# A transformer layer on eight cores: value weights loaded by halves of their columns, and the ternary scales taken at the end of two head pairs

## The chip, the cores and the metric

The kernel runs on the 8 NeuronCores of one Trainium2 chip. Every core does the whole layer for one of eight sequences, and no data passes between the cores. The metric is the device time of the slowest core in microseconds. Each core has five engines with an instruction queue of their own: PE (TensorE, matrix products), DVE (VectorE), ACT (ScalarE), POOL (GpSimd) and SP (SyncE, which only issues transfers here). The program is written engine by engine; engines wait for each other through semaphores, and nothing reorders the instructions of a queue.

## The reference

One pre-norm layer on x of 8 x 2048 x 1024: causal attention of 16 heads of 64, then a feed-forward part with quantized weights.

```python
x = x + attn(layernorm(x), W_query, W_key, W_value)      # causal softmax, 16 heads
x = x + ffn(layernorm(x), w1, conv_w, conv_b, w2)

def weight_quant(w):
    scale = 1.0 / clip(mean(abs(w)), 1e-05)
    return clip(round(w * scale), -1, 1) / scale          # ternary weights
def bit_linear(x, w):                                     # x by act_quant: 8 bits per token
    return einsum('bsd,hd->bsh', act_quant(x), weight_quant(w))
# ffn: h = bit_linear(x, w1); depthwise conv of width 3 over tokens; silu; bit_linear(h, w2)
```

## The kernel before

Tokens are worked in 16 tiles of 128 (`st` is the tile). The time falls into three stages.

**Values and first projections (0 to 104 us).** For each tile of x, DVE takes mean and variance (`moments`, L1218 to L1226), ACT forms the normalized tile `lnst` (`norm1`, L1019 to L1034, two buffers), PE turns it (`turn_ln`, L705, into `psTr`, two buffers), and DVE places it in `ln1T` (`place_ln`, L1231). PE then multiplies it by the value weights `Wvb` (`values`, L723): 8 matmuls for the left 512 columns (`nh` 0, heads 0 to 7) and 8 for the right ones. The results go round three PSUM banks `psV`; DVE copies the left half out (`place_v`, L1241), ACT the right half (`place_v`, L1049), both into `vaug`, whose columns of ones POOL writes once (L608). After every fourth tile PE projects a 512-token chunk to queries (`psQK`) and keys (`psK`) of the first head pair (`project`, L748).

The value weights are four transfers of 1 MB, each 256 rows of W_value by all 1024 columns (`load_wv`). Of each, ACT casts the first 128 rows to bf16 (L1041) and POOL the second (L597). `values` waits for all eight casts. SP issues the transfers in the order idbf, x0, wv0, wv1, x1, wv2, wv3, x2, x3, six constants, x4 to x15.

The query and key weights go another way. POOL itself issues their transfers (`load_wqk`, L502) into one staging buffer `wqkst`, casts them to bf16 (`cast_wqk`, L510 and L511), and only then issues the next one. The first issue stands in POOL's queue between its third and its fourth cast of value weights; `project` of the keys (`w` 1) waits for the second `cast_wqk`.

**Attention (104 to 468 us).** Eight head pairs (`hp` 0 to 7) of 40 slots each; slot `s` is one unit of 128 keys by up to 512 queries. In a slot PE forms scores (L806, from pair 3 on with a masking matmul L816), part of the next pair's projection (L748) and the weighted sum of an earlier unit (L834); ACT takes the exponential (L1110). Beside this DVE works through the feed-forward weights: 32 steps that sum absolute values (L1318), then 32 that make ternary weights (L1326, L1331), eight steps in a pair. The sums of each weight matrix become a scale in six small pieces: DVE `sum_columns` (L1338), PE `weight_sum` (L784), DVE `mean_weight` (L1344, L1348), PE `spread_scale_w` (L789, L791), DVE `place_scale` (L1353 to L1357). The PSUM bank `psN` that they use is shared with the norms of queries and keys, of which PE takes two sets in each pair (`norms`, L763, at slots 3 and 23, numbered `d`). So `norms(6)` and `norms(10)` wait until the scale is read out.

**Feed-forward (468 to 976 us).** 64 blocks of first products (L950), convolution on three engines, and second products (L968). The change doesn't touch this stage.

The order around the change is written out by hand in each engine's queue: the loops over `st` and over `slot` with comparisons against fixed slot numbers.

Of the kernel before, what the change touches and what calls it, by code (L numbers as in the profile page):

```python
# [16 lines left out]
S = 2048  # L17
D = 1024
# [37 lines left out]
def build_program():  # L56
# [24 lines left out]
    with es:  # L81
# [180 lines left out]

        BEFORE = {7: 0, 9: 1, 12: 2, 13: 3, 14: 4, 15: 5}
# [13 lines left out]
        def wv_quarter(n):  # L277

            return wvst[:, 2 * n * D:2 * (n + 1) * D]
# [84 lines left out]
        def _(e):  # L364
# [4 lines left out]
            def load_wv(n):  # L369
                e.dma_start(  # L370
                    out=wv_quarter(n).rearrange("p (c d) -> p c d", d=D),
                    in_=wv_h[256 * n:256 * (n + 1), :]
                    .rearrange("(c p) d -> p c d", p=128)
                ).then_inc(d_wv[n], 16)
# [122 lines left out]
        def _(e):  # L497
# [95 lines left out]
            def cast_wv(n):  # L593

                e.wait_ge(d_wv[n], 16)
                at = (2 * n + 1) * D
                e.tensor_copy(Wvb[:, at:at + D],  # L597
                              wvst[:, at:at + D]).then_inc(g_wv, 1)

            cast_wv(0)  # L600
            cast_wv(1)
# [5 lines left out]
            ap = vaug[:].rearrange("p (s h w) -> p (s h) w", h=H, w=VW)  # L607
            e.memset(ap[:, :, DH:DH + 1], 1.0).then_inc(g_vones, 1)  # L608
# [89 lines left out]
        def _(e):  # L698
# [10 lines left out]
            def values(st):  # L709
                e.wait_ge(v_lnT, st + 1)  # L710
                e.wait_ge(a_wv, 4)
                e.wait_ge(g_wv, 4)
                for nh in range(2):
                    n = 2 * st + nh
                    if n >= 3:

                        m = n - 3
                        if m % 2 == 0:
                            e.wait_ge(v_v, m // 2 + 1)
                        else:  # L720
                            e.wait_ge(a_v, m // 2 + 1)
                    for kc in range(8):
                        inst = e.matmul(  # L723
                            psV[n % 3][:],
                            ln1T[:, S * kc + 128 * st:S * kc + 128 * (st + 1)],
                            Wvb[:, D * kc + 512 * nh:D * kc + 512 * (nh + 1)],
                            start=(kc == 0), stop=(kc == 7))
                    inst.then_inc(t_v, 1)
# [25 lines left out]
            def norms(d):  # L754

                e.wait_ge(g_sq, 4 * (d + 1))
                if d >= 1:
                    e.wait_ge(a_c, d)
                if d in (6, 10):

                    e.wait_ge(v_fin, 3 if d == 6 else 6)
                for k in range(16):
                    inst = e.matmul(psN[:, k:k + 1],  # L763
                                    sqb[:, 128 * k:128 * (k + 1)],
                                    onesb[:, 0:1], start=True, stop=True,
                                    skip_group_check=True)
                inst.then_inc(t_nrm, 1)
# [13 lines left out]
            def weight_sum(f):  # L781
                e.wait_ge(v_fin, 3 * f + 1)
                e.wait_ge(a_c, 6 if f == 0 else 10)
                e.matmul(psN[0:1, 308:309], onesf[:, 0:1], smalls[:, 30:31],  # L784
                         start=True, stop=True).then_inc(t_fin, 1)
# [112 lines left out]
            for slot in range(NU + 6):  # L898
# [112 lines left out]
        def _(e):  # L1011
# [27 lines left out]
            def cast_wv(n):  # L1039
                e.wait_ge(d_wv[n], 16)  # L1040
                e.activation(out=Wvb[:, 2 * n * D:(2 * n + 1) * D],  # L1041
                             in_=wvst[:, 2 * n * D:(2 * n + 1) * D],
                             func=AF.Identity).then_inc(a_wv, 1)

            def place_v(st):
                n = 2 * st + 1
# [154 lines left out]
        def _(e):  # L1201
# [35 lines left out]
            def place_v(st):  # L1237
                n = 2 * st
# [220 lines left out]
            for slot in range(NU + 8):  # L1459
# [260 lines left out]
```

## Time and profile before

| | us |
|---|---|
| median of 3 runs | 978.73 (978.38 to 979.12) |
| the profiled execution | 977.3 |
| its span on the slowest core (core 5) | 975.7 |
| spans of all cores | 969.7 to 975.7 |
| PE / DVE / ACT / POOL busy in it | 889.0 / 711.9 / 697.3 / 620.6 |

The time of an execution is 1.6 us longer than the span of its slowest core. Share of busy time says which engine is full over the whole span (PE, 91%), not what holds it up in a given microsecond; for that the rows further down show, for single instructions, when they start, how long they take, and in square brackets how long their engine sat idle before them and what ended the wait. Unless a group says otherwise they are of core 5.

### The profile page before, as it was taken

The numbers are of one execution on the slowest core, as the hardware profiler recorded it, in microseconds if no ns is written. First come the engines' busy times: TensorE is split into PE (matmuls) and PEld (weight loads), VectorE is DVE, ScalarE is ACT, GpSimd is POOL, SyncE is SP. The second block draws the span as 40 slices with busy tenths as digits, with TensorE's granted clock in tenths as the row PEclk, the third lists the DMA queues.
The fourth block names the chain that finished last, engine by engine and source line by source line (L and its number), as shares of the span: only waits on it lengthen the run. The fifth ranks groups of instructions, "written<-read, shape, count | busy, mean of one in ns | idle before, by whom it ended". The sixth has DMA issues, their size and how long they took to land.

```text
span 975.7 us, 24133 instructions; the slowest of 8 cores (969.7 to 975.7 us)
## 1 busy us (share of the span) xinstructions
PE 889.0 (91%) x7516; PEld 538.3 (55%) x7516; DVE 711.9 (73%) x1173; ACT 697.3 (71%) x1108; POOL 620.6 (64%) x819
## 2 busy tenths in 40 slices
PE   1999899999999989998776699999999999999998
PEld 0454454555554545554654466666666666666443
DVE  2677665566666676669588988989899887877651
ACT  3554698889887888988988678678777777766300
POOL 2220648574655565545546978979799797978650
PEclk9999999999998999999989899999999999999999
DMA  8952666765876777774894323325343223332121
GB/s 262 331 169 91 233 222 214 237 215 181 255 247 218 223 243 250 231 238 191 243 313 162 108 67 118 139 92 173 109 133 128 89 94 124 108 130 88 44 87 44
DMA packets 38891, 166.93 MB, mean 171 GB/s; under 512 B 4977, under 2 KB 5106, under 8 KB 30066
## 3 DMA queue, kind: packets, MB, share of 16 engines
q1 hardware_dynamic: 34354, 148.62, 47.0%
q0 software_dynamic: 4416, 16.78, 5.1%
q8 instruction: 66, 1.08, 0.4%
q14 instruction: 55, 0.45, 0.2%
HBM read 140.22 MB, written 25.17 MB: 170 GB/s over the span
## 4 chain that ended last, share of the span: by engine, by line
PE 75%; DVE 7%; ACT 6%; issue 6%; DMA 3%; POOL 2%; SPq 0%; DVEq 0%; ACTq 0%; POOLq 0%
PE psO L968 21%; PE psM L950 19%; PE psQK L748 11%; PE psS L806 7%; PE psPV L834 6%; PE psV L723 5%; ACT PT L1110 4%; DMA wvst<-wv 2%; DMA w1b<-t1scr 2%; PE psS L816 1%; DVE psD L1543 1%; DVE hs L1524 1%; POOL hs L667 1%; PE psK L748 1%; ACT hs L1159 1%
## 5 line engine op out<-in xcount | busy, mean ns | idle before, releaser
L1110 ACT ACTIVATE PT<-psS,nbias 128x1024 bf16<-128x1024 f32 (+1 forms) x320 | 299.9, 986 | 45.2 <-PE psS L806 27.2
L950 PE MATMUL psM<-xqT,w1b 128*128 128x258 bf16 x2048 | 242.9, 277 | 20.3 <-DVE hs L1524 16.2
L667 POOL TENSOR_TENSOR hs<-hs,tb 128x256 f32<-128x256 f32 x256 | 194.6, 784 | 68.2 <-DVE hs L1524 61.8
L950 PEld LDWEIGHTS psM<-xqT,w1b 128*128 128x128 fp8e4 x2048 | 200.7, 99 | 61.4 <-issue 24.3
L1159 ACT ACTIVATE hs<-psM,convb_s,convw_s 128x256 f32<-128x256 f32 x256 | 147.5, 576 | 86.2 <-PE psM L950 61.4
L676 POOL TENSOR_TENSOR hs<-hs,srow 128x256 f32<-128x256 f32 x240 | 178.5, 777 | 15.5 <-ACT srow L1177 15.4
L1524 DVE SCALAR_TENSOR_TENSOR hs<-psM,convw_s,hs 128x256 f32<-128x256 f32 x256 | 114.8, 476 | 23.7 <-ACT tb L1163 22.6
L1543 DVE TENSOR_REDUCE psD<-hs 128x256 f32<-128x1024 f32 x56 | 109.3, 1952 | 22.0 <-ACT hs L1170 22.0
L748 PE MATMUL psQK<-ln1T,wqkb 128*128 128x512 bf16 x480 | 124.0, 382 | 1.4 <-ACT qkO L1086 0.2
L1163 ACT ACTIVATE tb<-psM,convw_s 128x256 f32<-128x256 f32 x256 | 123.6, 483 | 0.0
L834 PEld LDWEIGHTS psPV<-vaug,PT 128*128 128x128 bf16 x2176 | 92.1, 98 | 50.8 <-issue 25.5
L968 PE MATMUL psO<-w2T,hqa 128*128 128x512 fp8e4 x512 | 115.1, 379 | 0.6 <-DVE hqa L1590 0.6
L968 PE MATMUL psO<-w2T,hqb 128*128 128x512 fp8e4 x512 | 114.6, 379 | 0.0
L545 POOL TENSOR_TENSOR x<-x,ctx 128x128 f32<-128x128 f32 x128 | 82.6, 674 | 49.4 <-DVE ctx L1308 49.2
L834 PE MATMUL psPV<-vaug,PT 128*128 128x65 bf16 x2176 | 110.2, 195 | 3.1 <-DVE ctx L1308 1.3
L525 POOL TENSOR_TENSOR sqb<-qkE 128x512 bf16<-128x512 bf16 x32 | 36.8, 1150 | 74.1 <-DVE qkE L1249 51.0
L968 PEld LDWEIGHTS psO<-w2T,hqa 128*128 128x128 f16 x512 | 49.9, 98 | 56.2 <-issue 1.0
L968 PEld LDWEIGHTS psO<-w2T,hqb 128*128 128x128 f16 x512 | 50.1, 98 | 55.7
L1170 ACT ACTIVATE hs<-hs 128x1024 f32<-128x1024 f32 x64 | 68.8, 1075 | 15.6 <-POOL hs L667 15.5
L1318 DVE TENSOR_REDUCE smalls<-wbuf 128x1 f32<-128x2048 f32 x32 | 72.7, 2279 | 3.3 <-DMA wbuf<-w1q 2.1
L748 PEld LDWEIGHTS psQK<-ln1T,wqkb 128*128 128x128 bf16 x480 | 38.6, 97 | 51.3 <-issue 20.6
L806 PE MATMUL psS<-qkO 64*128 64x512 bf16 (+3 forms) x320 | 57.3, 353 | 9.7 <-ACT PT L1110 8.4
(147 smaller groups left out, 1052.8 us busy)
## 6 DMA issues: line engine op xcount, KB each, us to landing
wbuf<-w1q SPq DMA_DIRECT2D x32, 1024.0 KB, 6.3
wbuf<-w2p SPq DMA_DIRECT2D x32, 1024.0 KB, 6.7
w1b<-t1scr SPq DMA_DIRECT2D x64, 512.0 KB, 3.5
x<-x SPq DMA_DIRECT2D x16, 512.0 KB, 16.7
wqkst<-wqk POOLq DMA_DIRECT2D x16, 512.0 KB, 6.6
x1scr<-x POOLq DMA_DIRECT2D x4, 2048.0 KB, 10.0
x1g<-x1scr SPq DMA_DIRECT2D x16, 512.0 KB, 4.5
out<-x1g SPq DMA_DIRECT2D x16, 512.0 KB, 2.9
```

What stands on the lines that cost most here:

```text
L667: e.tensor_tensor(hs_quad(q)[:, part], hs_quad(q)[:, part], tb_quad(q)[:, part], ALU.add).then_inc(g_add, 1)
L676: inst = e.tensor_tensor(part, part, srow[:, at:at + GRP], ALU.mult)
L748: inst = e.matmul(bank[:], wqkb[:, at:at + 128], ln1T[:, x0:x0 + 512], start=(kc == 0), stop=(kc == 7))
L806: inst = e.matmul(bP[:, 512 * h + 128 * j:512 * (h + 1)], qk[64 * h:64 * (h + 1), k0:k0 + 128], qk[64 * h:64 * (h + 1), q0:q0 + n], start= ...
L834: inst = e.matmul(psPV[:, 512 * h + VW * m:512 * h + VW * (m + 1)], pt_unit(u)[:, p0:p0 + 128], vaug[:, v0:v0 + VW], start=(kc == 0 and m ...
L950: inst = e.matmul(psM[j][:, 0:GRP + 2], w1b[:, at:at + 128], xqT[:, x0:x0 + GRP + 2], start=(kc == 0), stop=(kc == 7))
L968: inst = e.matmul(psO[n][:], hq_of(g)[:, at:at + 128], w2T[:, D * kc + 512 * n: D * kc + 512 * (n + 1)], start=(kc == 0), stop=(kc == 31))
L1110: e.activation(out=pt_unit(u).rearrange("p (h w) -> p h w", w=512)[:, :, 128 * j:512], in_=psS[u % 2][:].rearrange("p (h w) -> p h w", w=512)[
L1159: e.activation(out=hs_quad(q)[:, GRP * j:GRP * (j + 1)], in_=psM[j][:, 2:GRP + 2], func=AF.Identity, scale=convw[:, 3 * hh + 2:3 * hh + 3] ...
L1163: e.activation(out=tb_quad(q)[:, GRP * j:GRP * (j + 1)], in_=psM[j][:, 0:GRP], func=AF.Identity, scale=convw[:, 3 * hh:3 * hh + 1]).then_i ...
L1524: e.scalar_tensor_tensor(sl, psM[j][:, 1:GRP + 1], convw[:, 3 * hh + 1:3 * hh + 2], sl, ALU.mult, ALU.add).then_inc(v_tap, 1)
L1543: done(e.tensor_reduce(psD[:, 0:GRP], rows, AX.X, ALU.max, apply_absolute_value=True))
```

## The change

**Value weights by halves of their columns.** `load_wv(n)` now takes 512 rows (`n % 2`) of 512 columns (`n // 2`), still 1 MB each, in pieces of 2 KB where they were 4 KB. So transfers 0 and 1 hold the left half for all rows, and 2 and 3 the right half. ACT and POOL still cast half of each transfer. SP issues x2 ahead of wv2 and wv3. PE runs `values` for one half at a time, in the order of `HALVES`: left halves of tiles 0, 1 and 2, which wait for four casts only, then the right halves of tiles 0 to 2, and from tile 3 on both halves of a tile. POOL writes the ones of tiles 0 to 2 right after its first cast, and the rest after the last cast. DVE and ACT follow: DVE places all three left halves ahead of `moments` 3 to 5, and ACT normalizes tile 2 ahead of the last two casts.

**Scales at the ends of pairs 2 and 4.** The six pieces move from slots 8 to 17 to slots 32 to 38, and `norms(7)` and `norms(11)` wait for them instead of `norms(6)` and `norms(10)`.

```diff
+        HALVES = [(0, 0), (1, 0), (2, 0), (0, 1), (1, 1), (2, 1)]
+        HALVES += [(st, nh) for st in range(3, NT) for nh in range(2)]
...
             def load_wv(n):
                 e.dma_start(
-                    out=wv_quarter(n).rearrange("p (c d) -> p c d", d=D),
-                    in_=wv_h[256 * n:256 * (n + 1), :]
+                    out=wvst[:, 2048 * n:2048 * (n + 1)].rearrange(
+                        "p (c d) -> p c d", d=512),
+                    in_=wv_h[512 * (n % 2):512 * (n % 2 + 1),
+                             512 * (n // 2):512 * (n // 2 + 1)]
                     .rearrange("(c p) d -> p c d", p=128)
...
             load_x(1)
+            load_x(2)
             load_wv(2)
             load_wv(3)
-            load_x(2)
             load_x(3)
...
+            ap = vaug[:].rearrange("p (s h w) -> p (s h) w", h=H, w=VW)
             cast_wv(0)
+            e.wait_ge(a_wv, 1)
+            e.wait_ge(g_wv, 1)
+            e.memset(ap[:, 0:3 * H, DH:DH + 1], 1.0).then_inc(g_vones, 1)
             cast_wv(1)
             cast_wv(2)
             load_wqk(0, 0)
             cast_wv(3)
             e.wait_ge(a_wv, 4)
             e.wait_ge(g_wv, 4)
-            ap = vaug[:].rearrange("p (s h w) -> p (s h) w", h=H, w=VW)
-            e.memset(ap[:, :, DH:DH + 1], 1.0).then_inc(g_vones, 1)
+            e.memset(ap[:, 3 * H:, DH:DH + 1], 1.0).then_inc(g_vones, 1)
...
-            def values(st):
+            def values(st, nh):
+                n = HALVES.index((st, nh))
                 e.wait_ge(v_lnT, st + 1)
-                e.wait_ge(a_wv, 4)
-                e.wait_ge(g_wv, 4)
+                e.wait_ge(a_wv, 2 * (nh + 1))
+                e.wait_ge(g_wv, 2 * (nh + 1))
...
             turn_ln(1)
+            values(0, 0)
+            turn_ln(2)
+            values(1, 0)
+            values(2, 0)
             for st in range(NT):
-                values(st)
-                if st + 2 < NT:
+                if st >= 3:
+                    values(st, 0)
+                values(st, 1)
+                if 1 <= st and st + 2 < NT:
                     turn_ln(st + 2)
...
             cast_wv(0)
             cast_wv(1)
             norm1(1)
+            norm1(2)
             cast_wv(2)
             cast_wv(3)
-            norm1(2)
-            e.wait_ge(g_vones, 1)
+            e.wait_ge(g_vones, 2)
...
             moments(2)
             place_ln(1)
+            place_ln(2)
             e.wait_ge(g_vones, 1)
+            place_v(0)
+            place_v(1)
+            place_v(2)
+            for st in range(3, 6):
+                moments(st)
+            e.wait_ge(g_vones, 2)
...
-                if d in (6, 10):
-                    e.wait_ge(v_fin, 3 if d == 6 else 6)
+                if d in (7, 11):
+                    e.wait_ge(v_fin, 3 if d == 7 else 6)
...
-                if (hp, s) in ((2, 11), (4, 11)):
+                if (hp, s) in ((2, 33), (4, 33)):
                     weight_sum(hp // 2 - 1)
-                if (hp, s) in ((2, 16), (4, 16)):
+                if (hp, s) in ((2, 37), (4, 37)):
                     spread_scale_w(hp // 2 - 1)
...
-                if (hp, s) in ((2, 8), (4, 8)):
+                if (hp, s) in ((2, 32), (4, 32)):
                     sum_columns(hp // 2 - 1)
-                if (hp, s) in ((2, 13), (4, 13)):
+                if (hp, s) in ((2, 35), (4, 35)):
                     mean_weight(hp // 2 - 1)
-                if (hp, s) in ((2, 17), (4, 17)):
+                if (hp, s) in ((2, 38), (4, 38)):
                     place_scale(hp // 2 - 1)
```

On PE, at the start of the program, the queue held before (`psTr0`, `psTr1` are the two buffers for turned tiles, `psV0` to `psV2` the three banks of values):

```order
L705 MATMUL psTr0<-idbf_s,lnst 128x128 x8
L705 MATMUL psTr1<-idbf_s,lnst 128x128 x8
L723 MATMUL psV0<-Wvb,ln1T 128x512 x8
L723 MATMUL psV1<-Wvb,ln1T 128x512 x8
L705 MATMUL psTr0<-idbf_s,lnst 128x128 x8
L723 MATMUL psV2<-Wvb,ln1T 128x512 x8
L723 MATMUL psV0<-Wvb,ln1T 128x512 x8
L705 MATMUL psTr1<-idbf_s,lnst 128x128 x8
```

and it holds now, at the same place:

```order
L727 MATMUL psTr0<-idbf_s,lnst 128x128 x8
L727 MATMUL psTr1<-idbf_s,lnst 128x128 x8
L744 MATMUL psV0<-Wvb,ln1T 128x512 x8
L727 MATMUL psTr0<-idbf_s,lnst 128x128 x8
L744 MATMUL psV1<-Wvb,ln1T 128x512 x8
L744 MATMUL psV2<-Wvb,ln1T 128x512 x8
L744 MATMUL psV0<-Wvb,ln1T 128x512 x8
L744 MATMUL psV1<-Wvb,ln1T 128x512 x8
L727 MATMUL psTr1<-idbf_s,lnst 128x128 x8
L744 MATMUL psV2<-Wvb,ln1T 128x512 x8
```

Tile 2 is turned after one half of values where it came after two, and tile 3 after five halves where it came after four. On POOL, behind the constants, the queue held before:

```order
L597 CAST Wvb<-wvst 128x1024 x3
L502 DMA wqkst<-wqk 128x1024
L597 CAST Wvb<-wvst 128x1024
L608 MEMSET vaug 128x256
L510 CAST wqkb<-wqkst 128x512
L511 CAST wqkb<-wqkst 128x512
```

and now:

```order
L614 CAST Wvb<-wvst 128x2x512
L623 MEMSET vaug 128x48
L614 CAST Wvb<-wvst 128x2x512 x2
L520 DMA wqkst<-wqk 128x1024
L614 CAST Wvb<-wvst 128x2x512
L630 MEMSET vaug 128x208
L528 CAST wqkb<-wqkst 128x512
L529 CAST wqkb<-wqkst 128x512
```

The issue of the first query weights has kept its place behind the third cast. On PE the scale of the first weights is spread (`spread_scale_w`) between full units of pair 2; before, with L806 scores, L748 projection and L834 weighted sums:

```order
L834 MATMUL psPV<-vaug,PT 128x65 x2
L806 MATMUL psS<-qkE 128x512 x2
L748 MATMUL psQK<-ln1T,wqkb 128x512 x4
L806 MATMUL psS<-qkE 128x512 x2
L789 MATMUL psN<-nrm,onesrow_s 128x1
L791 MATMUL psN<-nrm,onesrow_s 128x1
L806 MATMUL psS<-qkE 128x512 x2
L748 MATMUL psQK<-ln1T,wqkb 128x512 x4
```

and now it stands near the pair's end (L827 scores, L769 projection, L855 weighted sums):

```order
L827 MATMUL psS<-qkE 128x384 x2
L769 MATMUL psQK<-ln1T,wqkb 128x512 x4
L855 MATMUL psPV<-vaug,PT 128x65 x8
L810 MATMUL psN<-nrm,onesrow_s 128x1
L812 MATMUL psN<-nrm,onesrow_s 128x1
L827 MATMUL psS<-qkE 128x256 x2
L855 MATMUL psPV<-vaug,PT 128x65 x8
L827 MATMUL psS<-qkE 128x128 x2
```

These two instructions moved from full units to the short units on the diagonal.

## Rows read from the trace of the kernel before

**Rows 1.** The page, part 4: shares of the chain that ended last

```profile
PE 75%; DVE 7%; ACT 6%; issue 6%; DMA 3%; POOL 2%; SPq 0%; DVEq 0%; ACTq 0%; POOLq 0%
```

**Rows 2.** PE in order of time: start us, us, instruction [idle before <-releaser]

```profile
23.16 4.92 PE L723 MATMUL psV<-Wvb,ln1T 128*128 128x512 bf16 x16 [1.97 <-POOL Wvb L597]
27.92 0.61 PE L705 MATMUL psTr<-idbf_s,lnst 128*128 128x128 bf16 x8
28.37 3.62 PE L723 MATMUL psV<-Wvb,ln1T 128*128 128x512 bf16 x16
40.39 1.89 PE L748 MATMUL psQK<-ln1T,wqkb 128*128 128x512 bf16 x8
42.12 1.89 PE L748 MATMUL psK<-ln1T,wqkb 128*128 128x512 bf16 x8
```

**Rows 3.** POOL in order of time

```profile
19.88 0.75 POOL L502 DMA_DIRECT2D wqkst<-wqk  x1
29.57 0.61 POOL L510 CAST wqkb<-wqkst 128x512 bf16<-128x512 f32 x1 [5.23 <-DMA wqkst<-wqk]
31.32 0.55 POOL L502 DMA_DIRECT2D wqkst<-wqk  x1 [0.59 <-POOL wqkb L511]
40.96 0.62 POOL L511 CAST wqkb<-wqkst 128x512 bf16<-128x512 f32 x1
```

**Rows 4.** Core 4: PE at the first keys

```profile
43.41 1.89 PE L748 MATMUL psK<-ln1T,wqkb 128*128 128x512 bf16 x8 [0.35 <-POOL wqkb L511]
```

**Rows 5.** DVE in order of time, its wait for x2

```profile
23.37 0.69 DVE L1218 BATCH_NORM_STATS2 bn<-x 128x6 f32<-128x512 f32 x1 [5.02 <-DMA x<-x]
```

**Rows 6.** Core 5: us, then PE, PEld, DVE, ACT, POOL busy, PEclk, DMA share, GB/s

```profile
173.00:194.10 21.10, 20.16 (x228) 10.92 (x224) 12.11 (x17) 19.54 (x24) 10.33 (x16) 1.00 0.69 222
357.60:379.50 21.90, 21.07 (x245) 11.81 (x242) 15.12 (x21) 19.77 (x24) 8.80 (x8) 1.00 0.77 246
```

**Rows 7.** ACT and DVE around tile 4: place_v, norm1; a left half placed, moments

```profile
29.08 0.20 ACT L1019 ACTIVATE lnA<-lnA 128x1 f32<-128x1 f32 x1 [0.29 <-DVE lnA L1226]
30.11 1.24 ACT L1034 ACTIVATE lnst<-x,lnA 128x1024 bf16<-128x1024 f32 x1
...
26.47 0.70 DVE L1241 CAST vaug<-psV 128x512 bf16<-128x512 f32 x1 [0.56 <-PE psV L723]
27.07 0.68 DVE L1218 BATCH_NORM_STATS2 bn<-x 128x6 f32<-128x512 f32 x1
28.84 0.14 DVE L1226 TENSOR_SCALAR lnA<-lnA 128x1 f32<-128x1 f32 x1
```

**Rows 8.** PE at the scale pieces of pair 2 and at its end, DVE there

```profile
208.46 0.38 PE L789 MATMUL psN<-nrm,onesrow_s 1*128 1x1 f32 x2
209.00 0.39 PE L806 MATMUL psS<-qkE 64*128 64x512 bf16 x2
229.54 0.39 PE L806 MATMUL psS<-qkE 64*128 64x512 bf16 x2 [0.31 <-ACT PT L1110]
233.23 0.28 PE L806 MATMUL psS<-qkE 64*128 64x256 bf16 x2
...
228.40 4.47 DVE L1318 TENSOR_REDUCE smalls<-wbuf 128x1 f32<-128x2048 f32 x2
```

**Rows 9.** Core 5: first halves of pairs 1 and 2 (columns as in 6)

```profile
150.50:173.00 22.50, 20.66 (x240) 11.16 (x239) 14.99 (x23) 19.80 (x26) 18.24 (x32) 1.00 0.67 210
194.10:216.90 22.80, 21.23 (x247) 11.84 (x246) 15.48 (x29) 19.78 (x26) 18.28 (x32) 1.00 0.67 214
```

**Rows 10.** Pair 4: POOL, DVE, PE in order of time, and the clock

```profile
291.50 1.69 POOL L545 TENSOR_TENSOR x<-x,ctx 128x128 f32<-128x128 f32 x4
291.53 3.74 DVE L1331 TENSOR_SCALAR t8s<-t1s 128x2048 fp8e4<-128x2048 int16 x1 [0.17 <-DVE t1s L1326]
296.81 0.39 PE L806 MATMUL psS<-qkE 64*128 64x512 bf16 x2 [1.26 <-ACT PT L1110]
299.00:308.00 9.00, 9.00 (x74) 4.95 (x72) 5.31 (x7) 6.08 (x7) 8.17 (x8) 0.63 0.81 242
```

More of the change, by code:

```diff
@@ L257, in build_program, with half_bank @@
         block = es.enter_context(nc.Block())
+        HALVES = [(0, 0), (1, 0), (2, 0), (0, 1), (1, 1), (2, 1)]
+        HALVES += [(st, nh) for st in range(3, NT) for nh in range(2)]
+        def half_bank(st, nh):
+            return HALVES.index((st, nh)) % 3
         BEFORE = {7: 0, 9: 1, 12: 2, 13: 3, 14: 4, 15: 5}
@@ L275, in wbuf_landed, with wv_quarter, wvb_part @@
             e.wait_ge(d_wb[n % 2], 16 * (n // 2 + 1))
-        def wv_quarter(n):
-            return wvst[:, 2 * n * D:2 * (n + 1) * D]
+        def wv_quarter(n, half):
+            at = 4 * n + 2 * half
+            return wvst[:, 512 * at:512 * (at + 2)]
+        def wvb_part(Wvb, n, half):
+            kc = 4 * (n % 2) + 2 * half
+            return Wvb[:, D * kc:D * (kc + 2)].rearrange(
+                "p (c d) -> p c d", d=D)[
+                    :, :, 512 * (n // 2):512 * (n // 2 + 1)]
         def t8s_slot(i):
@@ L595, in cast_wv @@
                 e.wait_ge(d_wv[n], 16)
-                at = (2 * n + 1) * D
-                e.tensor_copy(Wvb[:, at:at + D],
-                              wvst[:, at:at + D]).then_inc(g_wv, 1)
+                e.tensor_copy(wvb_part(Wvb, n, 1),
+                              wv_quarter(n, 1).rearrange(
+                                  "p (c d) -> p c d", d=512)).then_inc(g_wv, 1)
+            ap = vaug[:].rearrange("p (s h w) -> p (s h) w", h=H, w=VW)
             cast_wv(0)
+            e.wait_ge(a_wv, 1)
+            e.wait_ge(g_wv, 1)
+            e.memset(ap[:, 0:3 * H, DH:DH + 1], 1.0).then_inc(g_vones, 1)
             cast_wv(1)
@@ L707, in turn_ln @@
                 inst.then_inc(t_lntr, 1)
-            def values(st):
+            def values(st, nh):
+                n = HALVES.index((st, nh))
                 e.wait_ge(v_lnT, st + 1)
-                e.wait_ge(a_wv, 4)
-                e.wait_ge(g_wv, 4)
[L713 to L728, printed above, removed]
+                e.wait_ge(a_wv, 2 * (nh + 1))
+                e.wait_ge(g_wv, 2 * (nh + 1))
+                if n >= 3:
+                    before, mh = HALVES[n - 3]
+                    if mh == 0:
+                        e.wait_ge(v_v, before + 1)
+                    else:
+                        e.wait_ge(a_v, before + 1)
+                for kc in range(8):
+                    inst = e.matmul(
+                        psV[n % 3][:],
+                        ln1T[:, S * kc + 128 * st:S * kc + 128 * (st + 1)],
+                        Wvb[:, D * kc + 512 * nh:D * kc + 512 * (nh + 1)],
+                        start=(kc == 0), stop=(kc == 7))
+                inst.then_inc(t_v, 1)
             def project(c, w, half, bank):
@@ L782, in weight_sum @@
                 e.wait_ge(v_fin, 3 * f + 1)
-                e.wait_ge(a_c, 6 if f == 0 else 10)
+                e.wait_ge(a_c, 7 if f == 0 else 11)
                 e.matmul(psN[0:1, 308:309], onesf[:, 0:1], smalls[:, 30:31],
@@ L1040, in cast_wv @@
                 e.wait_ge(d_wv[n], 16)
-                e.activation(out=Wvb[:, 2 * n * D:(2 * n + 1) * D],
-                             in_=wvst[:, 2 * n * D:(2 * n + 1) * D],
+                e.activation(out=wvb_part(Wvb, n, 0),
+                             in_=wv_quarter(n, 0).rearrange(
+                                 "p (c d) -> p c d", d=512),
                              func=AF.Identity).then_inc(a_wv, 1)
             def place_v(st):
-                n = 2 * st + 1
+                n = HALVES.index((st, 1))
                 e.wait_ge(t_v, n + 1)
@@ L1237, in place_v @@
             def place_v(st):
-                n = 2 * st
+                n = HALVES.index((st, 0))
                 e.wait_ge(t_v, n + 1)
@@ L1440, in _ @@
             place_ln(1)
+            place_ln(2)
             e.wait_ge(g_vones, 1)
+            place_v(0)
[4 more added lines that the diff above has]
+            e.wait_ge(g_vones, 2)
             for st in range(NT):
-                place_v(st)
-                if st + 3 < NT:
+                if st >= 3:
+                    place_v(st)
+                if st >= 3 and st + 3 < NT:
                     moments(st + 3)
-                if st + 2 < NT:
+                if st >= 1 and st + 2 < NT:
                     place_ln(st + 2)
```

## The prediction

> **What bounds the kernel now.** I read the chain of waits first. Three quarters of it are PE [rows 1], so the change pays where it shortens PE's own sequence or a wait in it. Then I read PE in order of time. It has turned tile 1 by 21.2, idles 1.97 us until 23.16 for POOL's last cast of value weights, and from there runs nearly without a gap: the first keys start at 42.12 [rows 2]. The whole stage behind them follows PE. Then POOL, because PE needs what it casts: right behind its third value cast the first query weights are issued at 19.88, they are cast from 29.57, the key weights are issued at 31.32, and their second cast runs from 40.96 to 41.58 [rows 3]. PE starts the keys at 42.12, 0.5 us later. On core 4 this slack is already gone: the row of the keys at 43.41 names POOL's L511 as what ended its wait [rows 4]. So two chains meet at the first keys: PE's own work, and POOL's two transfers one behind the other.
>
> **Part 1, the transfers.** x2 now goes ahead of wv2 and wv3. Before, POOL's last value weights had landed by about 21.9 and DVE's wait for x2 ended at 23.37 [rows 5], so 0.5 MB takes 1.5 us (1 MB: 3.0). wv2, for which POOL's third cast waits, lands 1.5 us later. Its pieces are also 2 KB where they were 4 KB. No row shows such loads. Below, they might cost nothing; above, a 2 KB piece might take as long as one of 4 KB, 3.0 us more for each MB. The nearest rows are two stretches of attention: without stores of 2 KB pieces DMA moves 222 GB/s at a share of 0.69, so 322 at full share; with them (a fifth of the bytes) 246 at 0.77, so 319 [rows 6]. That is 1% for a fifth, 5% for all, or 0.15 us for each MB. Three of them precede the third cast: 0.45. So the third cast, and the issue of the first query weights that stands behind it in POOL's queue, come 1.5 + 0.45 = 2.0 us later, at 21.9.
>
> The Trainium skill (DMA: Bandwidth & Descriptors, Specifications) asks for transfers of at least 512 B for line rate and names no loss at 2 KB. By it the 0.45 would be nothing. No run here shows the 2 KB loads yet.
>
> **POOL's chain.** From issue to cast the first transfer took 29.57 - 19.88 = 9.7 us and the second 40.41 - 31.32, with the cast of L510 ahead of L511, about 9.1 [rows 3]. x still fills the queues until the middle forties, so I take both durations as they are. The second cast then ends at 41.58 + 2.0 = 43.6, and PE may start the keys at 43.7 where they started at 42.12: 1.6 us later. On core 4, which had no slack, it is 2.0. Below, the durations may shrink, since the first transfer shares the queues with fewer value weights; I allow 2 us.
>
> **PE's own chain.** When could PE be there? x1 lands behind two MB, so 0.3 later. Turning tile 1 ends at 21.5. The left half of tile 0 starts at once, 1.7 us before 23.16 [rows 2]. At the lower of the clock's two levels (1.2 GHz) 8 matmuls take 3.4; at the higher 1.73 (42.12 - 40.39) [rows 2]. The first 16 took 4.92 where the next took 3.62, so they began low, and now that time lies under the left half of tile 0: 24.9. Turning tile 2, 0.8 low: 25.7. Four halves: 4 x 1.73 = 6.9, to 32.6. Now comes the turn of tile 3, and it needs ACT's `lnst`. DVE places the left half of tile 2 only when it is done (29.1), 0.6, and only then takes moments of tile 3, 1.9 (27.07 to 28.98): 31.6. ACT's chain from there takes 31.35 - 29.08 = 2.3 [rows 7]: 33.9. PE idles 1.3. Turn 0.45 and half 1.73: 36.1. ACT has placed a right half (0.6) and normalized tile 4 (2.3): 36.7. PE idles 0.6 more. Turn, two halves, turn: 4.35, to 41.1. Queries 1.73: 42.8. So even without POOL's chain PE reaches the first keys 0.7 us later than before: the head start of 1.7 is given back at tiles 3 and 4, which were prepared ahead before and now wait behind three left halves.
>
> The later of both, 43.7, decides: +1.6. Bounds: 0 (the chains both shorten by what I allowed) and +2.5 (2 KB loads dearer by twice what I took). Behind the keys the order of each engine is that of before, DVE and ACT wait for PE there, and nothing gives the time back up to attention.
>
> The rest of part 1 costs nothing: the ones of three tiles are written while POOL would wait for wv1; the later casts of wv2 and wv3 end by 25.3 and are needed at 29.1; the two ordered waits on banks are for copies that are 2 us old by then.
>
> **Part 2, the scales.** No instruction is added or removed. On PE the spreading takes 209.00 - 208.46 = 0.54 us, the sum 0.2. Before, the first half of pair 2 was 0.3 longer than that of pair 1 (22.80 to 22.50) [rows 9], so 0.3 is what both cost there. At slot 33 there is a wait of 0.31 for ACT right behind [rows 8] that takes up the sum. At slot 37 the units are short, ACT waits for PE, and the 0.54 counts in full. So +0.24 in a pair, twice: +0.5 at most; if ACT's slack takes it up, -0.6. The row nearest is that of pair 2 itself; with the part that ACT's waits take up I take +0.2. On DVE `mean_weight` stands behind the step of slot 34. Steps 34 and 39 run from 228.40 to 232.87 [rows 8], so the first ends at 230.6, and PE reaches the place of the spreading just ahead of its scores at 233.23: 2.6 us of cover. If DVE were later than that, the scores of slot 38, queued behind the waiting instruction, and ACT behind them would wait for the excess. `place_scale` holds step 39 back by 3 us, in time in which DVE was idle.
>
> **Sum.** Profiled execution 977.3 + 1.6 + 0.2 = 979.1. Against the median of the runs, which lies 1.4 above the profiled one, 978.73 + 1.8 = 980.5. A measurement of this kernel tells 0.2% (2.0 us) from no change; 980.5 is just inside it.
>
> **Rivals.**
> *POOL's transfers are not later* (chance 0.20). They get more of the queues as the value weights thin out. For it: 9.7 us for 0.5 MB is mostly waiting for others. Against it: the second took as long with other traffic. Then PE's chain decides, +0.7, and 978.73 + 0.7 + 0.2 = 979.6.
> *The head start stays* (0.12). Needs POOL's chain over 3 us shorter and ACT ahead of PE at tiles 3 and 4: -1.7, and with part 2 at its lower end -0.6: 976.4. Against it: tile 3's moments stand behind the third left half in DVE's queue.
> *The clock falls* (0.14), the slower side. PE now idles 1.3, 0.6 and 0.9 us within 12 us, where it had no gap. In pair 4 PE idled 1.26 us, and over the nine us from 299 on the granted clock was 0.63 in the mean, which is the lower level, 1.2 GHz, for most of them: 9 x 0.37 = 3.4 us of work lost, of which I count 2.7, as PE would have waited for ACT in part [rows 10]. It decides from such a fall on the slowest core: 980.5 + 2.7 = 983.2. Against it: ahead of each of the three gaps PE has worked for 2 us or more without one.
> *The collision in pair 4 goes* (0.09). DVE's L1331 takes 3.74 us there, 1.23 elsewhere, since POOL's additions start 0.03 us ahead of it [rows 10]; the 1.26 on PE follows. `sum_columns` leaves the queue ahead of it, so DVE could be first: -2.2, and 978.3. Against it: pair 5 has no such piece and collides too. The Trainium skill (SBUF — State Buffer, Who interferes with whom) says that the port pair that DVE and GpSimd share is held for a whole instruction by whichever issues first, the other blocking fully. By that rule the trace agrees: 3.74 ends behind POOL's work.
>
> **Chances.** Forecast 0.45 (0.23 inside 0.2%, 0.22 above it), POOL not later 0.20 (all inside), head start 0.12 (0.08 faster, 0.04 inside), clock 0.14 (slower), collision 0.09 (0.02 faster, 0.05 inside, 0.02 slower). Faster 0.10, same 0.52, slower 0.38. The forecast's own range is 979.3 to 981.6. The range for 8 in 10 reaches down to 978.0, which takes in the second rival and the collision, and up to 982.6, into the clock's case.
>
> **What would show it.** Right: POOL's first issue of query weights near 21.9, PE's first keys near 43.7 with POOL's L529 as what ended the wait, first scores about 105.6, gaps on PE ahead of the turns of tiles 3 and 4. Wrong: first keys at or before 42.1 (then both chains were overrated); a granted clock of 0.50 between 30 and 50 us; pair 2 or 4 longer or shorter by over 0.5 us; 2 KB loads that land over 0.5 us for each MB later.

## The result, and the profile after

| | before | after |
|---|---|---|
| median of 20 runs each | 978.28 us | 980.47 us |
| the profiled execution | 977.3 us | 979.8 us |
| spans of all cores in it | 969.7 to 975.7 us | 971.8 to 978.2 us |

The ratio is 1.0026, with a 95% interval of 1.0018 to 1.0034: 2.5 us slower, 1.8 to 3.3. It leaves out the executions, three of before and one of after, in which the cores of one die ran at a lower granted clock; the medians above, which include them, lie 2.2 us apart. The forecast was 980.5 us and 1.8 us slower. The slowest core is now core 4; rows of after are of core 4 unless the text says otherwise.

The chain that ended last, by engine and by line, from the page of after:

```profile
PE 72%; ACT 6%; issue 6%; DVE 6%; DMA 5%; POOL 3%; SPq 0%; DVEq 0%; ACTq 0%; POOLq 0%
PE psO L995 21%; PE psM L977 19%; PE psQK L769 9%; PE psS L827 7%; PE psPV L855 6%; ACT PT L1138 4%; PE psV L744 3%; DMA wqkst<-wqk 2%; DMA w1b<-t1scr 2%; DMA wvst<-wv 2%; PE psS L837 1%; DVE psD L1579 1%; PE psK L769 1%; POOL hs L689 1%; DVE hs L1560 1%
```

PE was 75% [rows 1] and is 72%. `DMA wqkst<-wqk`, the transfer of query and key weights, is in the chain with 2%: 21 us at the start of the program that the chain of core 4 now follows through POOL's transfers and no longer through PE.

PE of after in order of time, selected rows (start us, us, instruction, idle before it and what ended that), for [rows 2]:

```profile
20.15 3.62 PE L744 MATMUL psV<-Wvb,ln1T 128*128 128x512 bf16 x8
...
33.27 0.61 PE L727 MATMUL psTr<-idbf_s,lnst 128*128 128x128 bf16 x8 [1.79 <-ACT lnst L1061]
...
35.99 0.61 PE L727 MATMUL psTr<-idbf_s,lnst 128*128 128x128 bf16 x8 [0.40 <-ACT lnst L1061]
...
40.51 1.89 PE L769 MATMUL psQK<-ln1T,wqkb 128*128 128x512 bf16 x8
...
45.54 3.23 PE L769 MATMUL psK<-ln1T,wqkb 128*128 128x512 bf16 x8 [3.14 <-POOL wqkb L529]
```

The first values start at 20.15 where they started at 23.16 on core 5 (22.47 on core 4). Two gaps ahead of the turned tiles 3 and 4 take 2.2 us back. Then PE has its queries done at 42.4 and stands for 3.14 us, until POOL has cast the key weights. And the 8 matmuls behind that wait take 3.23 us, not 1.89. The granted clock tells why. The stretch 44 to 47 us of core 4 (us, then PE, PEld, DVE, ACT, POOL busy, PEclk, DMA share, GB/s):

```profile
44.00:47.00 3.00, 1.46 (x4) 0.59 (x5) 0.00 (x0) 0.00 (x0) 2.20 (x4) 0.65 1.06 354
```

0.65 is a mean of the two levels, so the clock was at the lower one, 1.2 GHz, for most of this stretch. In steps of half a microsecond it reads 1.00 up to 44.5, 0.87 in the next step and 0.50 from 45.0 to 48.0: it fell in the wait, and the keys pay for it.

POOL of after, for [rows 3]:

```profile
19.92 1.04 POOL L614 CAST Wvb<-wvst 128x1024 bf16<-128x1024 f32 x1 [5.37 <-DMA wvst<-wv]
20.91 0.75 POOL L520 DMA_DIRECT2D wqkst<-wqk  x1
...
31.61 0.61 POOL L528 CAST wqkb<-wqkst 128x512 bf16<-128x512 f32 x1 [5.79 <-DMA wqkst<-wqk]
...
33.36 0.55 POOL L520 DMA_DIRECT2D wqkst<-wqk  x1 [0.59 <-POOL wqkb L529]
...
44.77 0.62 POOL L529 CAST wqkb<-wqkst 128x512 bf16<-128x512 f32 x1
```

The first issue is at 20.91 (19.88 on core 5 of before), the second cast starts at 44.77 (40.96 there). The key weights alone took 10.9 us from issue to cast on this core.

One core is one draw, so here is the same for all eight: the mean over the cores of one profiled execution each.

| us | before | after |
|---|---|---|
| first values start | 23.10 | 20.68 |
| POOL's third value cast starts | 18.82 | 19.98 |
| first transfer, issue to cast | 10.9 | 9.8 |
| second transfer, issue to cast | 9.0 | 10.0 |
| POOL's cast of the key weights ends | 42.63 | 43.70 |
| PE's first keys | 43.16 | 43.94 |
| PE idle ahead of them | 0 to 0.45 | 0 to 3.14 |
| first scores, mean (last core) | 105.06 (105.99) | 105.89 (108.66) |

The first stage is not the whole story of these two executions. The mean span of the eight cores grew by 2.7 us, from 972.7 to 975.4: 0.8 of it up to the first scores, 0.6 in pairs 0 to 3, 0.9 in pairs 4 and 5, and 0.4 behind them. Cores 6 and 7 of after had their first scores at 105.3 and 105.2, yet they ended at 977.9 and 978.1, level with core 4. In pairs 4 and 5 the granted clock fell for some microseconds on two cores of the profile before and on five of the profile after. Nothing ties that to the change: it fell there on five cores of `before_wqk_early` further down too, which has neither part.

**Part 2 on core 5.** The norms that open pairs 2, 3 and the second half between them, first of before, then of after:

```profile
194.13 0.55 PE L763 MATMUL psN<-onesb_s,sqb 128*128 128x1 bf16 x16
...
216.87 0.54 PE L763 MATMUL psN<-onesb_s,sqb 128*128 128x1 bf16 x16
...
238.33 0.54 PE L763 MATMUL psN<-onesb_s,sqb 128*128 128x1 bf16 x16
```

```profile
195.85 0.55 PE L784 MATMUL psN<-onesb_s,sqb 128*128 128x1 bf16 x16
...
218.32 0.54 PE L784 MATMUL psN<-onesb_s,sqb 128*128 128x1 bf16 x16
...
240.30 0.54 PE L784 MATMUL psN<-onesb_s,sqb 128*128 128x1 bf16 x16
```

First half 22.74 before, 22.47 after; second half 21.46 before, 21.98 after. The pieces leave 0.27 behind where they were and cost 0.52 where they stand now: +0.25 in pair 2. In pair 4 core 5 can't serve, since its clock fell there in the kernel before (27.74 in the first half). The medians of the cores are 25.08 and 21.92 before, 24.85 and 22.49 after: +0.34. But single cores lie far from them, from 23.62 to 25.95 in the first half of after, so this second figure is weaker.

**The collision of pair 4** stays as it was [rows 10] on seven of the eight cores. POOL's addition, then DVE's L1359:

```profile
296.62 1.69 POOL L563 TENSOR_TENSOR x<-x,ctx 128x128 f32<-128x128 f32 x4
```

```profile
296.65 3.74 DVE L1359 TENSOR_SCALAR t8s<-t1s 128x2048 fp8e4<-128x2048 int16 x1 [0.17 <-DVE t1s L1354]
```

On core 6 of after the instruction took 1.23, PE idled 0.64, and the first half of pair 4 took 23.62. So whether DVE and POOL meet there differs between cores of one program.

### The profile page after: what moved, and what is told of

It is laid out like the page before. It is cut to its first block, busy times and chain, and to the rows that moved or that the text cites. A ratio compares the mean times of both kernels' runs of the same rounds, so it can differ in the third digit from the quotient of the medians.

```text
span 978.2 us, 24119 instructions; the slowest of 8 cores (971.8 to 978.2 us)
## 1 busy us (share of the span) xinstructions
PE 879.9 (90%) x7450; PEld 537.4 (55%) x7516; DVE 712.6 (73%) x1173; ACT 697.1 (71%) x1108; POOL 620.9 (63%) x820
## 4 chain that ended last, share of the span: by engine, by line
PE 72%; ACT 6%; issue 6%; DVE 6%; DMA 5%; POOL 3%; SPq 0%; DVEq 0%; ACTq 0%; POOLq 0%
PE psO L995 21%; PE psM L977 19%; PE psQK L769 9%; PE psS L827 7%; PE psPV L855 6%; ACT PT L1138 4%; PE psV L744 3%; DMA wqkst<-wqk 2%; DMA w1b<-t1scr 2%; DMA wvst<-wv 2%; PE psS L837 1%; DVE psD L1579 1%; PE psK L769 1%; POOL hs L689 1%; DVE hs L1560 1%
## 5 line engine op out<-in xcount | busy, mean ns | idle before, releaser
L769 PE MATMUL psQK<-ln1T,wqkb 128*128 128x512 bf16 x429 | 111.8, 379 | 8.6 <-issue 4.6
L855 PEld LDWEIGHTS psPV<-vaug,PT 128*128 128x128 bf16 x2176 | 91.1, 97 | 50.1 <-issue 24.7
L855 PE MATMUL psPV<-vaug,PT 128*128 128x65 bf16 x2176 | 109.2, 194 | 3.7 <-ACT PT L1138 1.6
L769 PEld LDWEIGHTS psQK<-ln1T,wqkb 128*128 128x128 bf16 x480 | 38.5, 97 | 51.1 <-issue 20.2
L827 PE MATMUL psS<-qkO 64*128 64x512 bf16 (+3 forms) x320 | 57.3, 353 | 9.6 <-ACT PT L1138 8.3
```

What stands on the lines that cost most here:

```text
L769: inst = e.matmul(bank[:], wqkb[:, at:at + 128], ln1T[:, x0:x0 + 512], start=(kc == 0), stop=(kc == 7))
L827: inst = e.matmul(bP[:, 512 * h + 128 * j:512 * (h + 1)], qk[64 * h:64 * (h + 1), k0:k0 + 128], qk[64 * h:64 * (h + 1), q0:q0 + n], start= ...
L855: inst = e.matmul(psPV[:, 512 * h + VW * m:512 * h + VW * (m + 1)], pt_unit(u)[:, p0:p0 + 128], vaug[:, v0:v0 + VW], start=(kc == 0 and m ...
```

## The experiments

The first four kernels ran on one chip, with the kernel before at a median of 979.84 us (35 runs); the last four together on another, with it at 978.16 us (23 runs). Each is judged by its ratio to the kernel before beside it; `after_x2_late` ran once and is read for its rows alone. Where it helps, a second measure stands beside the ratio: the span of an execution as the mean of its eight cores, which leans less on the worst one, with its 95% interval, against the kernel before of the same session.

**Each part alone: `p1_only`.** Part 2 undone in the kernel after.

```diff
-                if (hp, s) in ((2, 33), (4, 33)):
+                if (hp, s) in ((2, 11), (4, 11)):
                     weight_sum(hp // 2 - 1)
...  (likewise 37 to 16, 32 to 8, 35 to 13, 38 to 17; norms(7), (11) to (6), (10) and the count that weight_sum waits for)
```

> Part 1 alone (values by halves), the scales at their old slots. Theory (POOL's chain of two transfers decides the first keys, and part 2 costs 0.5 us): first keys as in the changed kernel, 1 to 3 us after those of before on most cores; time of before + 1.9 us, ratio 1.0019. Rival (most of the loss is the moved scales): time within 0.5 us of before, ratio below 1.0006.

Measured: median 983.41, ratio 1.0029 (1.0014 to 1.0045). Part 1 alone is slower, by 2.8 us (1.4 to 4.4); the mean span of the cores is 2.0 us longer (1.4 to 2.7). So it can be most or all of the whole. The profiled execution, 986.4 us, lies 3 us above the median: all eight cores wait 1.78 to 4.76 us for the key weights, and on four of them the keys take 2.9 to 3.3 us. Those four are not simply the ones that waited longest. Core 5, then core 7:

```profile
45.92 3.18 PE L769 MATMUL psK<-ln1T,wqkb 128*128 128x512 bf16 x8 [2.25 <-POOL wqkb L529]
```

```profile
45.10 1.89 PE L769 MATMUL psK<-ln1T,wqkb 128*128 128x512 bf16 x8 [3.10 <-POOL wqkb L529]
```

Core 5 waited 2.25 us and its clock fell some 0.4 us into the keys; core 7 waited 3.10 us and kept its full clock. Core 6, PE and then its clock:

```profile
33.84 0.61 PE L727 MATMUL psTr<-idbf_s,lnst 128*128 128x128 bf16 x8 [1.78 <-ACT lnst L1061]
...
47.73 3.29 PE L769 MATMUL psK<-ln1T,wqkb 128*128 128x512 bf16 x8 [4.76 <-POOL wqkb L529]
```

```profile
47.00:51.00 4.00, 3.27 (x9) 1.25 (x10) 0.00 (x0) 0.00 (x0) 2.16 (x4) 0.63 1.05 357
```

The same first stage ran in the kernel after with keys at 43.94 in the mean of the cores, here at 45.85. So the wait varies by 2 us between executions, and one profile doesn't fix its size.

**`p2_only`.** The same edit the other way, in the kernel before.

```diff
-                if (hp, s) in ((2, 11), (4, 11)):
+                if (hp, s) in ((2, 33), (4, 33)):
                     weight_sum(hp // 2 - 1)
...  (likewise 16 to 37, 8 to 32, 13 to 35, 17 to 38; norms(6), (10) to (7), (11))
```

> Part 2 alone (scales at the ends of pairs 2 and 4), values as before. Theory: the spreading counts in full among the short units, +0.25 in each of the two pairs, so second halves of pairs 2 and 4 are 0.5 us longer and first halves 0.25 shorter; time of before + 0.5 us, ratio 1.0005. Rival (moved to a quieter place): pairs 2 and 4 shorter by 0.3 each, ratio 0.9994.

Measured: ratio 1.0004 (0.9989 to 1.002). By its time this run decides nothing: the effect is smaller than its interval. The mean span of the cores is 0.9 us longer (0.1 to 1.7), so part 2 does cost something. The rows of pair 2 say how much. Core 0:

```profile
194.50 0.55 PE L763 MATMUL psN<-onesb_s,sqb 128*128 128x1 bf16 x16
...
216.96 0.54 PE L763 MATMUL psN<-onesb_s,sqb 128*128 128x1 bf16 x16
...
239.10 0.54 PE L763 MATMUL psN<-onesb_s,sqb 128*128 128x1 bf16 x16
```

22.46 and 22.14. Over the cores (medians) the first half of pair 2 is 0.27 shorter and the second 0.68 longer: +0.4. In pair 4 the second half is 0.52 longer, but the first is 0.24 and 0.29 shorter on two cores only (24.84 and 24.79) and takes 25.15 to 27.54 on the other six, where the clock fell or PE waited longer. So +0.3 for pair 4 is not shown by this run. Its first stage is that of before, yet its cores wait 0 to 2.37 us ahead of the keys, where in the profile of before the most was 0.45. That is the spread of an unchanged stage.

**Is it POOL's issue? `after_wqk_early`.** The first query weights are issued one cast earlier in the kernel after.

```diff
             cast_wv(1)
-            cast_wv(2)
             load_wqk(0, 0)
+            cast_wv(2)
             cast_wv(3)
```

> The changed kernel with POOL's issue of the first query weights ahead of its third value cast, so behind wv1 and not behind wv2. Theory: both transfers end about 5 us earlier, the wait ahead of the first keys is gone on every core, PE's own chain decides: first keys at 41.5 to 43.5, first scores near 104.5 to 105.5, time of before + 1.0 us, ratio 1.0010. Rival (the gaps ahead of tiles 3 and 4 and the scales make the whole loss): time as the changed kernel, ratio 1.0026.

Measured: ratio 0.9997 (0.9985 to 1.001), so the loss is gone; the mean span of the cores is 0.1 us shorter (-0.5 to +0.3). The kernel after ran in an earlier session, so the two ratios are what is compared. Core 4, PE:

```profile
33.52 0.61 PE L727 MATMUL psTr<-idbf_s,lnst 128*128 128x128 bf16 x8 [1.79 <-ACT lnst L1061]
...
42.48 1.89 PE L769 MATMUL psK<-ln1T,wqkb 128*128 128x512 bf16 x8
```

and POOL:

```profile
15.61 0.75 POOL L520 DMA_DIRECT2D wqkst<-wqk  x1
26.23 1.04 POOL L614 CAST Wvb<-wvst 128x1024 bf16<-128x1024 f32 x1 [4.16 <-DMA wvst<-wv]
...
40.62 0.62 POOL L529 CAST wqkb<-wqkst 128x512 bf16<-128x512 f32 x1
```

No core waits ahead of the keys; they start at 42.98 in the mean, at their full clock. The gap of 1.79 stays (1.69 on core 3), and on cores 1, 3 and 7 the second gap is no longer 0.40 but 1.19, 2.30 and 1.23, with DVE's copy `ln1T` as releaser: there DVE had waited 1.3 to 2.4 us for a tile of x, which lands later now. PE's own chain is what decides, and it ends where that of before ended, at 42.98 against 43.16. So the wait for POOL is what made the change slower, and the gaps are what keep it from being faster.

**The same line in the kernel before: `before_wqk_early`.**

> The kernel before with the same single move on POOL. Theory: the 0.35 to 0.45 us of waiting ahead of the first keys on two cores goes, but the 0.5 MB now travel ahead of wv3 and x2, the last value cast and with it the first values come up to 1.5 us later: time of before + 0.5 to + 1.5 us, ratio 1.0005 to 1.0015. Rival (POOL's chain is the bound in the kernel before as well): faster by 0.4 us, ratio 0.9996.

Measured: ratio 1.0007 (0.9994 to 1.002), no gain; the mean span of the cores is 1.2 us longer (0.6 to 1.9), so it is a loss. The transfer takes its share of the queues from the last value weights, and PE needs those first. Core 7, POOL's cast and then PE, its one row of first values and the keys:

```profile
24.55 1.04 POOL L597 CAST Wvb<-wvst 128x1024 bf16<-128x1024 f32 x1 [3.78 <-DMA wvst<-wv]
```

```profile
25.82 6.57 PE L723 MATMUL psV<-Wvb,ln1T 128*128 128x512 bf16 x16 [3.90 <-POOL Wvb L597]
...
46.40 1.89 PE L748 MATMUL psK<-ln1T,wqkb 128*128 128x512 bf16 x8
```

The first values start at 25.00 in the mean (23.10 before), the first scores at 107.13 (105.06). The order by halves is what makes this transfer harmless: with it PE has left halves to work on while the late weights land.

**What x2 costs and what the pieces cost: `after_x2_late`.**

```diff
             load_x(1)
-            load_x(2)
             load_wv(2)
             load_wv(3)
+            load_x(2)
```

> The changed kernel with x2 issued behind wv3 again. Theory (x2 in front of wv2 costs the third cast 1.5 us, and 2 KB pieces 0.15 us for each MB): POOL's third cast about 1.3 us earlier than in the changed kernel, near 18.8 on the mean of the cores against 19.98; but tile 2 is then normalized late, PE idles some 3 us ahead of turning it, and the first keys are no earlier than 43.5. Rival (2 KB pieces made the third cast late): the third cast stays within 0.4 us of 19.98.

Measured: one run, 984.25 us. POOL's third value cast starts at 18.43 in the mean of the cores; in the kernel after it is 19.98, so x2 ahead of it is worth 1.55 us (1.5 was forecast). In the kernel before, with the same transfers ahead of it in 4 KB pieces, it is 18.82. The 2 KB pieces landed no later. Both readings carry the spread between executions: 18.57 to 19.17 in the three profiles that load as before (18.57, of `before_bias`, on the same chip), 19.98 and 20.71 in the two that load as after. Turning tile 2 now waits for x2, on each core. Core 4, PE:

```profile
27.94 1.01 PE L727 MATMUL psTr<-idbf_s,lnst 128*128 128x128 bf16 x8 [3.68 <-ACT lnst L1061]
...
39.38 0.61 PE L727 MATMUL psTr<-idbf_s,lnst 128*128 128x128 bf16 x8 [1.79 <-ACT lnst L1061]
...
48.35 1.89 PE L769 MATMUL psK<-ln1T,wqkb 128*128 128x512 bf16 x8
```

Keys at 48.36 in the mean and without a wait in front of them: this kernel is bound by PE's chain, with both gaps in it.

**Closing the gaps too: `p1_wqk_ahead`.** Part 1 with the early issue and the old scales; DVE takes the moments of tile 3 right behind the first left half, and ACT normalizes tiles 3 to 5 one place earlier.

```diff
             norm1(2)
             cast_wv(2)
             cast_wv(3)
+            norm1(3)
             e.wait_ge(g_vones, 2)
             for st in range(NT):
                 place_v(st)
-                if st + 3 < NT:
+                if st < 2:
+                    norm1(st + 4)
+                elif 3 <= st < NT - 3:
                     norm1(st + 3)
...
             place_v(0)
+            moments(3)
             place_v(1)
             place_v(2)
-            for st in range(3, 6):
-                moments(st)
+            moments(4)
+            moments(5)
```

> Part 1 alone, with POOL's first issue of query weights ahead of its third value cast, and with tile 3 prepared ahead: DVE takes its moments right behind the first left half, ACT normalizes it ahead of the first right half, and tiles 4 and 5 follow one step ahead. Theory (the two gaps give back the head start): both gaps, 1.79 and 0.40 us, go; first keys near 40.8, first scores near 102.6 on the mean of the cores, 2.4 us ahead of before; ratio 0.9975. Rival (the early transfer or ACT's order makes a new gap): first scores no earlier than 104.

Measured: ratio 0.9986 (0.9975 to 0.9997), 1.4 us faster than the kernel before. The kernel leaves part 2 out; with it the gain would be some 0.6 us less, an estimate from the rows of part 2 above. First scores at 103.16 in the mean (105.06 before). On core 3 the whole stretch runs without a gap:

```profile
24.58 7.46 PE L744 MATMUL psV<-Wvb,ln1T 128*128 128x512 bf16 x32
31.88 0.61 PE L727 MATMUL psTr<-idbf_s,lnst 128*128 128x128 bf16 x8
...
40.35 1.89 PE L769 MATMUL psK<-ln1T,wqkb 128*128 128x512 bf16 x8
```

On the others a gap of 0.6 to 2.3 us is left a tile or two later, with another cause. Core 0, PE and then DVE:

```profile
34.50 0.61 PE L727 MATMUL psTr<-idbf_s,lnst 128*128 128x128 bf16 x8 [2.08 <-DVE ln1T L1262]
```

```profile
25.55 0.69 DVE L1249 BATCH_NORM_STATS2 bn<-x 128x6 f32<-128x512 f32 x1 [0.93 <-DMA x<-x]
...
29.70 0.69 DVE L1249 BATCH_NORM_STATS2 bn<-x 128x6 f32<-128x512 f32 x1 [1.01 <-DMA x<-x]
...
33.79 0.69 DVE L1262 COPY ln1T<-psTr 128x1024 bf16<-128x1024 bf16 x1
```

DVE waits for x3 and again for a later tile of x, which are loaded beside the early query weights, and its copy of a turned tile stands behind those moments in its queue. It is the transfers again: what is taken forward there is paid by x.

**The collision of pair 4: `before_bias`.** DVE's second step of a pair moves two slots later, in the kernel before.

```diff
-            STEPS += [UN * hp + s for s in (4, 9, 15, 19, 24, 29, 34, 39)]
+            STEPS += [UN * hp + s for s in (4, 11, 15, 19, 24, 29, 34, 39)]
```

> The kernel before with the second weight step of each pair at slot 11 where it was at slot 9, so behind the bias that ACT's exponentials of slots 12 and on wait for. Theory (DVE's 3.74 us step in pairs 4 and 5 holds the bias back and makes PE's wait of 1.26 us there): that wait goes, the first halves of pairs 4 and 5 fall from 25.1 and 24.9 to 23.0 to 23.5 us; time of before - 3 us, ratio 0.997. Rival (the step only moves its delay to another slot, ctx and the next tile waiting for it): pairs 4 and 5 within 0.5 us of before.

Measured: ratio 0.9981 (0.9968 to 0.9994), 1.9 us faster. The first half of pair 4 takes 23.87 to 24.04 us on five cores (25.01 to 25.35 on seven before), and that of pair 5 takes 23.6 on four (24.78 to 24.89 on five before). Core 1, DVE and PE:

```profile
290.45 2.63 DVE L1289 TENSOR_SCALAR nbias<-cbc 128x2 f32<-128x2 f32 x1 [0.68 <-ACT cbc L1098]
293.00 1.27 DVE L1326 TENSOR_SCALAR t1s<-wbuf,smalls 128x2048 int16<-128x2048 f32 x1
294.45 1.23 DVE L1331 TENSOR_SCALAR t8s<-t1s 128x2048 fp8e4<-128x2048 int16 x1 [0.17 <-DVE t1s L1326]
```

```profile
296.29 0.39 PE L806 MATMUL psS<-qkE 64*128 64x512 bf16 x2 [0.64 <-ACT PT L1110]
```

L1331 is back at 1.23, and PE idles 0.64 where it idled 1.26 [rows 10]. On the five cores a tiny instruction of 2 columns stands behind POOL now and takes 2.62 to 2.80 us; on core 1 it ends at 293.08, as POOL's square behind the additions ends at 293.06. It isn't shown to be the cause of the 0.64 that is left: on cores 4 and 5 it took 0.17, and PE idled 0.64 all the same, in halves of 24.97 and 24.77. Core 2, whose clock fell, took 26.76. Part of the gain may be the clock: in the first halves of pairs 4 and 5 it fell on one core of this profile, on two of the profile before, on four of `p1_only` and on five of `before_wqk_early`, whose attention is that of before. How much of the 1.9 us that makes stays open.

**All of it: `best`.** The edits of `p1_wqk_ahead` and of `before_bias` together.

> Both of the last two together: part 1 with the early issue and tile 3 ahead, scales at their old slots, and the second weight step at slot 11. Theory: the gains add, since the stages follow each other: before - 5.4 us, ratio 0.9945. Rival (one of them fails): ratio above 0.997.

Measured: median 973.72, ratio 0.9955 (0.9942 to 0.9968), 4.4 us faster than the kernel before, and faster than the kernel after by more. Singly the two gave 0.14% and 0.19%, together 0.45%; the intervals of the single ones reach 0.25% and 0.32%, so the sum is within what they allow. First scores 103.32, first half of pair 4 23.89. Two lines of its spans; all cores lie in 965.1 to 972.1:

```profile
core 1: 972.1 us, clock 0.987
core 3: 965.1 us, clock 0.992
```

## Why the prediction was right, point by point

- *x2 ahead of wv2, 1.5.* Right as far as one pair of profiles can say: 19.98 - 18.43 = 1.55, where profiles of one order of loads differ by 0.6 to 0.7.
- *2 KB pieces, 0.45.* Not seen: 18.43 against 18.57 to 19.17 in the three profiles with 4 KB pieces, where 0.45 more was expected. My estimate read 1% out of two stretches of attention that differ in more than the stores. The rule of the Trainium skill (DMA: Bandwidth & Descriptors, Specifications), line rate from 512 B up, agrees with this trace; the term should have gone by it. So the third cast came 1.16 later in the profile of after, and 1.5 in the mean of the profiles of each order, not 2.0.
- *POOL's two transfers keep their lengths.* Right in the sum only: in the means 10.9 and 9.0 became 9.8 and 10.0. The first took 9.8 to 10.9 in the profiles of either order, so its 1.1 is no effect of the change. The second took 9.0 to 9.5 in the three profiles that load as before and 10.0 and 10.2 in the two that load as after: it got longer by nearly 1 us, which I had not counted, and no run says why. POOL's chain ended 1.07 later; 2.0 was forecast.
- *PE's own chain, gaps of 1.3 and 0.6.* Right in place and cause, 1.79 and 0.40 on all cores, each with ACT's `lnst` as releaser. DVE's moments behind the third left half and ACT's chain of 2.3 give them; `p1_wqk_ahead`, which takes tile 3 ahead, has neither on core 3. The end of the chain was overrated. The 42.8 was worked out for core 5, which had 42.12 before: +0.7. With the wait for POOL removed (`after_wqk_early`), keys start at 42.25 on core 5, +0.1, and at 42.98 in the mean against 43.16, -0.2. The head start that the gaps give back was 2.4 in the mean, not 1.7.
- *First keys +1.6.* Half right. In the one profile +0.8 in the mean of the cores and +3.4 from the slowest core of before to that of after. The mean over the three profiles with the first stage of before (before, `p2_only`, `before_bias`) is 43.4, over the two with that of after (after, `p1_only`) 44.9: +1.5. That is near 1.6, but the means of single profiles run from 42.8 to 44.1 and from 43.9 to 45.9, and `p1_only` was profiled in an execution 3 us above its median, so the size stays between these figures. I treated as a fixed offset what is a wait that varies by 2 us from one execution to the next, and the time of a run is that of its slowest core. Both chains were overrated by 0.6 to 0.9 in the profile of after; what the slowest core adds was not in my sum.
- *The rival of the clock.* I gave it 0.14 as a case apart. It came true inside the forecast, and with it one of my signs of being wrong, a granted clock of 0.50 between 30 and 50 us: on core 4 the clock fell during the 3.14 us, and the keys took 1.34 us longer; in `p1_only` on four cores. Behind the two small gaps it didn't come: the matmuls behind 1.79 and 0.40 ran at full clock. The wait for POOL on a core without slack was the third and largest gap, and I had sized it at 0.9. The case I took as a model was a draw too: in pair 4 of before PE idled 1.2 to 1.4 us on all eight cores, and the clock fell on core 5 alone, whose first half took 27.74, 2.7 more than the median. (9 x 0.37 is 3.3, not 3.4; the 2.7 that I counted is what it cost.)
- *Part 2, +0.2.* Mis-sized: +0.6 by the rows of the kernel after (0.25 and 0.34), the second of them uncertain, and 0.9 (0.1 to 1.7) by the mean span of `p2_only`. Its upper bound, 0.5, was nearer. Nothing of the spreading is covered at slot 37; the 0.27 saved ahead is the 0.3 that I had read from [rows 9]. DVE's cover held: no wait of PE for `mean_weight` appears.
- *The collision goes, 0.09.* Out: 3.74 as before on seven cores, and `before_bias` shows what does move it.
- *The sum.* Part 1 alone measured +2.8 (1.4 to 4.4), where 1.6 stood; part 2 +0.6 from its rows, where 0.2 stood; the whole +2.5 (1.8 to 3.3), where 1.8 stood. Over the same two groups of profiles the first scores go from 105.3 to 107.2, +1.9, and 1.9 + 0.6 = 2.5; with profiles that differ by 2 us this agreement is no proof. That the forecast of 980.5 met the median of 980.47 is luck: the kernel before ran 0.45 us faster in the later runs than the median that I had started from, and the change cost about as much more than I had forecast. What the runs do show of the mechanism is that the two chains meet at the first keys, that POOL's decides there (`after_wqk_early` takes the loss away), and that PE's gaps give back its head start.

Open: why a transfer of 0.5 MB from POOL takes 9 to 11 us and differs by 2 us between executions of one stage. On core 4 the DMA engines were busy 0.97 of the time from 33 to 44 us and moved 305 GB/s, 2.8 MB on SP's queue beside 0.5 MB on POOL's, so sharing is the likely reason, but no run took x away. Open too is what makes the clock fall behind one wait and not behind a longer one.

## What to carry to other kernels

- When two chains meet at one instruction, a head start on one of them is worth only the slack of the other. Here PE started 2.4 us earlier in the mean and the same edit moved POOL's transfer 1.2 later; both had to be moved, and then a third thing, the tiles prepared ahead, had to follow.
- A transfer issued earlier is paid by the one that it passes: the same line gained about 2.9 us on the kernel after (ratios 1.0026 and 0.9997) and cost 1.2 us of the cores' mean span on the kernel before. Ask what PE can work on while the delayed one lands.
- Read a wait that ends on a transfer on all cores and in more than one profile before giving it a size.

## What the runs showed of the hardware

- The granted clock fell in or right behind single waits of PE of 3.14 us (kernel after) and of 2.25, 4.03, 4.41 and 4.76 us (`p1_only`), and the 8 matmuls behind them took 2.9 to 3.3 us for 1.89. It held behind waits of 2.78, 2.96 and 3.10 us in that same execution of `p1_only`, and behind gaps of 1.79 us. So the length of the wait alone doesn't tell.
- The same wait can cost the clock on one core and not on the next: with 1.2 to 1.4 us of idle time in pair 4 it fell on one of eight cores in the kernel before (27.74 us for the half instead of 25.08) and on four in `p1_wqk_ahead` (28.03 to 28.15).
- 1 MB of weights in pieces of 2 KB landed as soon as in pieces of 4 KB (18.43 for the third cast, against 18.57 to 19.17).
- Started just behind POOL's additions, even a DVE instruction of 2 columns took 2.63 us (`nbias`, core 1 of `before_bias`), and 0.17 on cores where it came ahead of them.
